# Attention: scores two units at a time, transposes one unit behind, context products between them

## The chip, the cores and the metric

The kernel runs on one core of a Trainium2 chip. The metric is the device time of one execution in microseconds (us), lower is better. Engines: PE is TensorE (matrix), with PEld for its weight loads; DVE is VectorE; ACT is ScalarE; POOL is GpSimd; SP issues the DMAs.

## The reference, cut to what matters

Four graph layers run one after another on 8 batch elements of 1024 nodes with 256 features. The change lies in the last one, attention with 8 heads of 32 features, in which the adjacency matrix (added to itself) multiplies the scores before the softmax:

```
q, k, v = proj(Wq, bq), proj(Wk, bk), proj(Wv, bv)          # [b, 8, 1024, 32]
scores = einsum('bhqd,bhkd->bhqk', q, k) * 32 ** -0.5
scores = scores * (adj + adj)[:, None, :, :]
attn = softmax(scores, axis=-1)
ctx = einsum('bhqk,bhkd->bhqd', attn, v)
x = layernorm(x + ctx @ Wo.T + bo)
```

## The kernel before, in words

The program treats the 8 batch elements one after another; each passes through the four layers, all on one core. Every engine has its own instruction list, written out by hand, and runs it in that order; semaphores tie the lists together. So the order of PE's work is the order of the Python loop in `@block.tensor`, and nothing reorders it.

In attention a *unit* is one query tile (128 rows, 8 tiles) of one head (8 heads): 64 units for an element, unit u being tile u // 8 and head u % 8. A unit's way:

- `scores` (L724): two matmuls of 512 columns on PE into two score banks. There are two such pairs of banks, used in turn, so unit u waits for `masked` of unit u - 2.
- DVE, L1530: one custom instruction multiplies the 128 x 1024 scores by the adjacency rows, writes them to one of three slots `r`, and gives their row maximum. POOL negates the maximum (L498).
- ACT, L1177: exponential in place, with the row sum.
- `transpose_p` (L734): eight transposes of 128 x 128 on PE into two banks, one for the lower four key tiles and one for the upper four. Each waits until its bank's copy of the unit before is done (`p_dve`, `p_act`).
- DVE L1546 copies the lower bank to `pt_0`, ACT L931 the upper one to `pt_1` or `pt_2`.
- `context` (L752): for a group of four heads, 16 small products per part, 32 instruction records, with the values; part 0 takes the lower keys, part 1 the upper ones. Groups 2 qt and 2 qt + 1 belong to query tile qt and both write bank 6 (the last group another). Before part 0 of the first group of a tile overwrites this bank, it waits for `c_raw`: DVE's product `c_f` (L1562) of the tile before.

Once per query tile there are also: the reciprocals of the row sums (DVE L1557), their spread over the partitions (`spread_denominators`, PE L765) and ACT's copy of it; `c_f` = context x spread reciprocals (DVE L1562); its split into high and low parts (ACT, POOL); the output projection (`output`, PE L506 to L508, bank 7); the residual addition into `xr` (DVE L1577), which needs the projection and waits for its own end; the statistics for the layer norm (DVE L1289, L1294); the normalisation (POOL, ACT), and the store.

Every engine's loop counts a step s. In PE's loop before, step s issues the scores of unit s + 1, the transposes of unit s - 2, part 0 of a group when s - 7 is a multiple of 4, part 1 when s - 9 is, the spread at s = 12, 20, ..., and the output projection at s = 16, 24, .... In steps 1 to 3 the values of two node tiles each are projected as well, between scores and transposes. DVE's step s has the masking product of unit s, in steps 1 to 3 the copy of the projected values (L1504), the copy of unit s - 2 (`LAG` is 2), the reciprocal at s = 8, 16, ..., `c_f` at s = 14, 22, ..., the residual addition at s = 17, 25, ..., and the statistics at s = 18, 26, .... ACT's step has the copy of unit s - 2, then the exponential of unit s. After the loop's last units PE already transposes adjacency tiles of the next element (L595).

Of the kernel before, what the change touches and what calls it, by code (L numbers as in the profile page):

```python
# [22 lines left out]
def build_program(nc: bass.Bass, d: dict, out: bass.AP):  # L23
# [7 lines left out]
    G = P // HD  # L31
    UNITS = NT * H
    EPS_DEG, EPS_ROW, EPS_LN = 1e-6, 1e-12, 1e-5
    SLOPE = 0.2
    LAG = 2
# [53 lines left out]
    with ExitStack() as ctx:  # L89
# [194 lines left out]
        def nth(b, per, n):  # L284

            return b * per + n
# [216 lines left out]
        def _(pe):  # L503
# [83 lines left out]
            def transpose_adj(b, j, half):  # L587

                n = tp["adj", j, half]
                tp_wait(b, n)  # L590
                for t in range(TPH):
                    i = TPH * half + t
                    if j == 0:
                        pe.wait_ge(adj_in[i], nth(b, 16, 16))
                    last = pe.transpose(tp_bank(n)[:, t * P:(t + 1) * P], adjn[:, i, j * P:(j + 1) * P], ident)  # L595
                last.then_inc(tp_full, 1)
# [50 lines left out]
            def project_pairs(b, name, w, rows_ready, pairs=range(PAIRS)):  # L647

                for k in pairs:
                    pe.wait_ge(*rows_ready(k))  # L650
                    dst = pr_bank(b, pr[name, k])
                    for s in range(2):
                        last = project(dst[:, s * F:(s + 1) * F], w, 2 * k + s)
                    last.then_inc(pr_full, 1)
# [19 lines left out]
            def xt_wait(b, layer):  # L674
                return lambda k: (tp_free, nth(b, TP_UNITS, x_ready(layer, 2 * k + 1)))
# [15 lines left out]
            def copied(b, n):  # L691

                pe.wait_ge(copies_dve if n % 2 else copies_act, nth(b, 2 * G, n // 2 + 1))

            def stack_copies(b, n):

                h, m, half = COPIES[n]
                pe.wait_ge(pr_free, nth(b, PR_UNITS, pr["qk", (0, m, half)] + 1))
                if 4 <= n < 3 * G or n >= 3 * G + 2:
                    copied(b, n - (4 if n < 3 * G else 2))  # L700
                at = slice(half * 512, (half + 1) * 512)
                block = lambda k, count: placer[:, (4 * h + k) * HD:(4 * h + k + count) * HD]
                dst = copies_bank(n)
                if m == 0:
                    pe.matmul(dst, block(2, 3), qk0_hi[:, 0, at], start=True, stop=False)
                    last = pe.matmul(dst, block(0, 3), qk0_lo[:, 0, at], start=False, stop=True)
                else:
                    pe.matmul(dst, block(1, 3), qk0_hi[:, 1, at], start=True, stop=False)
                    last = pe.matmul(dst, block(3, 3), qk0_lo[:, 1, at], start=False, stop=True)
                last.then_inc(copies_full, 1)  # L710

            def scores(b, u):
                qt, h = divmod(u, H)
                if u == 0:
                    copied(b, 3 * G - 2)
                    copied(b, 3 * G - 1)
                if u < G:
                    copied(b, 3 * G + u)
                if G <= u < 2 * G:
                    pe.wait_ge(stacked[u - G], nth(b, 16 * 6, 16 * 6))  # L720
                if u >= 2:
                    pe.wait_ge(masked, nth(b, UNITS, u - 1))
                for half in range(HALVES):
                    last = pe.matmul(ps[:, 2 * (u % 2) + half, :], q_stack[0:STACK, h, qt * P:(qt + 1) * P],  # L724
                                     k_stack[0:STACK, h, half * 512:(half + 1) * 512], start=True, stop=True)
                last.then_inc(s_full, 1)

            def transpose_p(b, u):
                pe.wait_ge(exp_done, nth(b, UNITS, u + 1))
                for half in range(HALVES):  # L730
                    if u >= 1:
                        pe.wait_ge(p_dve if half == 0 else p_act, nth(b, UNITS, u))
                    for t in range(TPH):
                        last = pe.transpose(ps[:, TP + half, t * P:(t + 1) * P],  # L734
                                            r[:, u % RSLOTS, (TPH * half + t) * P:(TPH * half + t + 1) * P], ident)
                    last.then_inc(p_full, 1)

            def context(b, grp, part):

                qt, g = divmod(grp, 2)  # L740
                if part == 0:
                    pe.wait_ge(p_dve, nth(b, UNITS, G * grp + G))
                    if grp == 0:
                        pe.wait_ge(pr_free, nth(b, PR_UNITS, PR_UNITS))
                    elif g == 0:
                        pe.wait_ge(c_raw, nth(b, NT + 1, qt))
                else:
                    pe.wait_ge(p_act, nth(b, UNITS, G * grp + G))
                for kt in range(TPH * part, TPH * (part + 1)):
                    for hh in range(G):  # L750
                        h = g * G + hh
                        last = pe.matmul(ps[HD * hh:HD * (hh + 1), ctx_bank(grp), g * P:(g + 1) * P],  # L752
                                         xn[:, kt, h * HD:(h + 1) * HD], p_half(grp * G + hh, kt // TPH)[:, kt % TPH, :],
                                         start=(kt == 0), stop=(kt == NT - 1), tile_position=(0, HD * hh))
                last.then_inc(ctx_done if part else ctx_half, 1)

            def spread_denominators(b, qt):

                pe.wait_ge(rp_ready, nth(b, NT, qt + 1))
                if qt >= 1:  # L760
                    pe.wait_ge(h_sum, nth(b, NT, qt))
                for g in range(2):
                    for hh in range(G):
                        h = g * G + hh
                        last = pe.matmul(ps[HD * hh:HD * (hh + 1), 7, g * P:(g + 1) * P],  # L765
                                         rprow[:, qt % 2, h:h + 1].broadcast_to([P, HD]), ident[:, :],
                                         start=True, stop=True, tile_position=(0, HD * hh))
                last.then_inc(rbc_full, 1)

            def output(b, qt):  # L770
                for g in range(2):
                    pe.wait_ge(c_ready, nth(b, NT + 1, NT + g if qt == NT - 1 else qt + 1))
                    last = three(ps[:, 7, 0:F], c_hi[:, g, :], c_lo[:, g, :], w_hi[:, W_O, g, :], w_lo[:, W_O, g, :],
                                 g == 0, g == 1)
                last.then_inc(o_full, 1)
# [4 lines left out]
            for b in range(B):  # L780
# [121 lines left out]
                    stack_copies(b, n)  # L902
                scores(b, 0)
                for s in range(UNITS + 10):
                    if s + 1 < UNITS:
                        scores(b, s + 1)
                    if s == 0:
                        for n in range(3 * G + 2, 4 * G):
                            stack_copies(b, n)
                    if 1 <= s < PAIRS:  # L910
                        project_pairs(b, "values", W_V, xt_wait(b, 3), range(s, s + 1))
                    if LAG <= s < UNITS + LAG:
                        transpose_p(b, s - LAG)
                    for part in range(2):
                        grp, late = divmod(s - 7 - 2 * part, G)
                        if late == 0 and 0 <= grp < 2 * NT:
                            context(b, grp, part)
                    if s in (UNITS + 1, UNITS + 5) and b + 1 < B:
                        for j in ((0, 1) if s == UNITS + 1 else (2, 3)):
                            transpose_adj(b + 1, j, 0)  # L920
                    if s >= 12 and (s - 12) % H == 0 and (s - 12) // H < NT - 1:
                        spread_denominators(b, (s - 12) // H)
                    if s == UNITS + 2:
                        spread_denominators(b, NT - 1)
                    if s >= 16 and (s - 16) % H == 0 and (s - 16) // H < NT:
                        output(b, (s - 16) // H)
# [274 lines left out]
        def _(dve):  # L1201
# [41 lines left out]
            def x_late_transposed(b, layer, part):  # L1243
                for (n, lo, src), (_, hi, _) in zip(x_late(layer, part, xt_lo), x_late(layer, part, xt_hi)):
                    dve.wait_ge(tp_hi, nth(b, TP_UNITS, n + 1))
                    rest(lo, src, hi, tp_free)
# [359 lines left out]
```

## Time and profile before

| | us |
|---|---|
| median of 3 runs | 3124.4 (3123.82 to 3126.77) |
| profiled execution | 3123.78 |
| its span, first to last instruction | 3122.0 |
| PE busy | 3021.2 (97%) |
| DVE busy | 2089.0 (67%) |
| ACT busy | 1718.1 (55%) |
| mean granted TensorE clock | 0.996 of full speed |

The busy time of an engine is summed over its instructions; matmuls are pipelined, and their ends are modelled. The chain that ended last goes from the last instruction backwards, at each step to what released it; groups in it are counted from the end of the one before to their own end, and so leave no overlap. Durations in the order of time overlap, since a matmul's weight load and its start lie beside the one before.

### The profile page before, as it was taken

To read this page: it belongs to the slowest core of one execution; us is meant where nothing else is said; L and a number is where in the kernel's file an instruction comes from. 1 tells how busy PE (TensorE), PEld (TensorE's weight loads), DVE (VectorE), ACT (ScalarE), POOL (GpSimd) and SP (SyncE) were. 2 spreads that over 40 slices of the span, in tenths; PEclk is the share of its full clock that TensorE was granted. 3 is DMA by queue.
4 is the path that set the end of the run, shared out by engine and by line. 5 is a ranking of instruction groups with operands and counts; after the bars stand their busy time and mean duration, and the time that the engine had idled before them with its cause. 6 is when DMAs were issued, how large, how long until landed. Compare 5 with 4: busy or idle time off the path is not lost.

```text
span 3122.0 us, 71133 instructions
## 1 busy us (share of the span) xinstructions
PE 3021.2 (97%) x28188; PEld 2645.0 (85%) x28188; DVE 2089.0 (67%) x4060; ACT 1718.1 (55%) x3048; POOL 448.6 (14%) x1666
## 2 busy tenths in 40 slices
PE   6999999999999999999999999999999999999999
PEld 5988889887898788987889977898778987789877
DVE  4637976379762797627976389753887538874388
ACT  3525854258542684526854278533785337853377
POOL 0101211012110121101211112111121111211112
PEclk9999999999999999999999999999999999999999
DMA  6022131121321213302133021330213302133110
GB/s 219 30 80 65 49 146 51 60 70 44 144 78 37 67 52 136 103 15 67 49 136 109 13 70 44 134 109 14 69 53 125 109 17 70 49 126 109 27 40 19
DMA packets 145270, 234.50 MB, mean 75 GB/s; under 512 B 12839, under 2 KB 113964, under 8 KB 144940
## 3 DMA queue, kind: packets, MB, share of 16 engines
q1 hardware_dynamic: 144940, 229.96, 22.7%
q8 instruction: 225, 3.69, 0.5%
q14 instruction: 105, 0.86, 0.1%
HBM read 120.86 MB, written 83.89 MB: 66 GB/s over the span
## 4 chain that ended last, share of the span: by engine, by line
PE 87%; DVE 5%; ACT 3%; SPq 2%; issue 1%; POOL 1%; DMA 0%; DVEq 0%; POOLq 0%; ACTq 0%
PE ps L506 17%; PE ps L508 16%; PE ps L507 16%; PE ps L734 15%; PE ps L724 9%; PE ps L752 8%; DVE t_lo L1233 2%; SPq L409 1%; PE ps L605 1%; PE ps L765 1%; PE ps L564 1%; ACT t_hi L931 1%; PE ps L595 1%; DVE xt_lo L1240 0%; DVE stats L1289 0%
## 5 line engine op out<-in xcount | busy, mean ns | idle before, releaser
L1530 DVE CUSTOM_DVE_ANT_0 r<-ps,adjn 128x1024 f32<-128x1024 f32 x512 | 620.7, 1212 | 19.0 <-DVE xr L1577 10.3
L1177 ACT ACTIVATE r<-r,nmax 128x1024 f32<-128x1024 f32 x512 | 584.8, 1142 | 23.0 <-POOL nmax L498 22.8
L506 PE MATMUL ps<-u_hi,t_hi 128*128 128x256 f32 x2048 | 588.6, 287 | 2.4 <-DVE t_lo L1233 1.8
L508 PE MATMUL ps<-u_hi,t_lo 128*128 128x256 f32 x2048 | 579.4, 283 | 0.0
L507 PE MATMUL ps<-u_lo,t_hi 128*128 128x256 f32 x2048 | 578.9, 283 | 0.0
L734 PEld LDWEIGHTS ps<-ident,r 128*128 128x128 f32 x4096 | 462.5, 141 | 116.0 <-issue 78.1
L734 PE MATMUL ps<-ident,r 128*128 128x128 f32 x4096 | 536.7, 274 | 7.9 <-DVE pt L1546 7.5
L1546 DVE COPY pt<-ps 128x512 f32<-128x512 f32 x512 | 352.9, 689 | 93.6 <-PE ps L734 74.2
L931 ACT ACTIVATE pt<-ps 128x512 f32<-128x512 f32 x512 | 304.0, 594 | 176.6 <-PE ps L734 160.4
L506 PEld LDWEIGHTS ps<-u_hi,t_hi 128*128 128x128 f32 x2048 | 391.4, 191 | 6.2 <-DVE t_lo L1233 6.2
L507 PEld LDWEIGHTS ps<-u_lo,t_hi 128*128 128x128 f32 x2048 | 391.4, 191 | 0.0
L508 PEld LDWEIGHTS ps<-u_hi,t_lo 128*128 128x128 f32 x2048 | 391.2, 191 | 0.0
L724 PE MATMUL ps<-k_stack,q_stack 96*128 96x512 f32 x1024 | 363.3, 437 | 6.1 <-ACT k_stack L931 4.3
L1006 ACT ACTIVATE xn<-y,shift,rstd 128x256 f32<-128x256 f32 x192 | 115.6, 602 | 456.8 <-POOL shift L474 456.0
L506 PE MATMUL ps<-w_hi,xt_hi 128*128 128x256 f32 x1152 | 334.4, 290 | 18.5 <-DVE xt_lo L1240 8.7
L507 PE MATMUL ps<-w_lo,xt_hi 128*128 128x256 f32 x1152 | 323.1, 280 | 0.0
L508 PE MATMUL ps<-w_hi,xt_lo 128*128 128x256 f32 x1152 | 322.7, 280 | 0.0
L467 POOL TENSOR_TENSOR vare<-mv,eps_ln 128x1 f32<-128x1 f32 x256 | 53.5, 209 | 1589.9 <-DVE mv L1294 1589.9
L752 PE MATMUL ps<-pt,xn 128*32 128x128 f32 x8192 | 274.9, 275 | 0.0
L1233 DVE TENSOR_TENSOR xt_lo<-ev,xt_hi 128x512 fp32r<-128x512 f32 x64 | 44.3, 693 | 316.4 <-ACT xt_hi L931 316.4
L506 PEld LDWEIGHTS ps<-w_hi,xt_hi 128*128 128x128 f32 x1152 | 218.5, 190 | 36.5 <-issue 13.4
L498 POOL TENSOR_TENSOR nmax<-zero,mmax 128x1 f32<-128x1 f32 x512 | 97.1, 190 | 1036.7 <-DVE mmax L1530 991.2
(164 smaller groups left out, 5235.8 us busy)
## 6 DMA issues: line engine op xcount, KB each, us to landing
adjn<-in_adj SPq DMA_DIRECT2D x64, 512.0 KB, 3.5
t_spill<-t_hi SPq DMA_DIRECT2D x64, 512.0 KB, 5.8
t_spill<-t_lo SPq DMA_DIRECT2D x64, 512.0 KB, 5.9
t_hi<-t_spill SPq DMA_DIRECT2D x32, 1024.0 KB, 5.3
t_lo<-t_spill SPq DMA_DIRECT2D x32, 1024.0 KB, 8.3
xn<-in_x SPq DMA_DIRECT2D x16, 512.0 KB, 4.5
x_spill<-xn SPq DMA_DIRECT2D x64, 128.0 KB, 1.7
q_stack<-u_hi SPq DMA_DIRECT2D x64, 128.0 KB, 2.5
```

Source lines behind the costliest of these rows:

```text
L506: pe.matmul(dst, a_hi, b_hi, start=first, stop=False, skip_group_check=check)
L507: pe.matmul(dst, a_hi, b_lo, start=False, stop=False, skip_group_check=check)
L508: return pe.matmul(dst, a_lo, b_hi, start=False, stop=last, skip_group_check=check)
L724: last = pe.matmul(ps[:, 2 * (u % 2) + half, :], q_stack[0:STACK, h, qt * P:(qt + 1) * P], k_stack[0:STACK, h, half * 512:(half + 1) * 512 ...
L734: last = pe.transpose(ps[:, TP + half, t * P:(t + 1) * P], r[:, u % RSLOTS, (TPH * half + t) * P:(TPH * half + t + 1) * P], ident)
L752: last = pe.matmul(ps[HD * hh:HD * (hh + 1), ctx_bank(grp), g * P:(g + 1) * P], xn[:, kt, h * HD:(h + 1) * HD], p_half(grp * G + hh, kt // ...
L931: copy = lambda dst, src, scale=1.0: nc.scalar.activation(dst, src, ACT.Copy, scale=scale)
L1006: act.activation(dst, src, ACT.Identity, bias=shift[:, t % 4:t % 4 + 1], scale=rstd[:, t % 4:t % 4 + 1]).then_inc(ln_done, 1)
L1177: act.activation(r[:, s % RSLOTS, :], r[:, s % RSLOTS, :], ACT.Exp, bias=nmax[:, s % 4:s % 4 + 1], accum_out=prow[:, qt % 2, h:h + 1]).the ...
L1233: dve.tensor_tensor(dst, value, f32(hi), ALU.subtract).then_inc(done, 1)
L1530: dve.tensor_tensor_reduce(out=r[:, s % RSLOTS, :], in0=ps[:, 2 * (s % 2):2 * (s % 2) + 2, :].rearrange("p a c -> p (a c)"), in1=adjn[:, q ...
L1546: dve.tensor_copy(p_half(u, 0).rearrange("p t q -> p (t q)"), ps[:, TP, :]).then_inc(p_dve, 1)
```

## The change

Only PE's instruction order in the attention loop is different. Scores are issued for two units in each odd step (s + 1 and s + 2; in step 0 for unit 1), the transposes are those of unit s - 1 instead of s - 2, and the context parts stand two steps earlier (s - 5 and s - 7 multiples of 4). A pair of steps before was: scores, transposes, scores, transposes, context. After, it is: scores, scores, transposes, context; transposes. The spread and the output projection keep their step numbers, and so do all lists of the other engines.

```diff
                 scores(b, 0)
                 for s in range(UNITS + 10):
-                    if s + 1 < UNITS:
-                        scores(b, s + 1)
+                    for u in (1,) if s == 0 else (s + 1, s + 2) if s % 2 else ():
+                        if u < UNITS:
+                            scores(b, u)
                     if s == 0:
                         for n in range(3 * G + 2, 4 * G):
                             stack_copies(b, n)
                     if 1 <= s < PAIRS:
                         project_pairs(b, "values", W_V, xt_wait(b, 3), range(s, s + 1))
-                    if LAG <= s < UNITS + LAG:
-                        transpose_p(b, s - LAG)
+                    if 1 <= s <= UNITS:
+                        transpose_p(b, s - 1)
                     for part in range(2):
-                        grp, late = divmod(s - 7 - 2 * part, G)
+                        grp, late = divmod(s - 5 - 2 * part, G)
                         if late == 0 and 0 <= grp < 2 * NT:
                             context(b, grp, part)
```

## Rows read from the trace of the kernel before

**Rows 1.** The page: busy time of the engines; shares of the chain by engine.

```profile
PE 3021.2 (97%) x28188; PEld 2645.0 (85%) x28188; DVE 2089.0 (67%) x4060; ACT 1718.1 (55%) x3048; POOL 448.6 (14%) x1666
PE 87%; DVE 5%; ACT 3%; SPq 2%; issue 1%; POOL 1%; DMA 0%; DVEq 0%; POOLq 0%; ACTq 0%
```

**Rows 2.** Busy time in one stretch: PE, PEld, DVE, ACT, POOL, granted clock, DMA.

```profile
350.00:400.00 50.00, 50.00 (x675) 39.64 (x674) 45.40 (x84) 42.14 (x79) 11.34 (x41) 1.00 0.12 39
```

**Rows 3.** Chain of waits, one block of 8 units: start us, us, what.

```profile
305.61 0.57 PE ps L765 x16
306.18 0.66 PE ps L724 x2
306.84 0.87 PE ps L734 x8
307.71 1.01 PE ps L752 x32
...
310.26 0.47 PE ps L724 x2
310.73 1.04 PE ps L734 x8
...
314.32 0.12 PE ps L506
...
315.03 0.47 PE ps L724 x2
...
316.38 1.01 PE ps L752 x32
...
323.02 0.57 PE ps L765 x16
```

**Rows 4.** Order of time, a later block: start us, us, engine, line, what, idle before.

```profile
344.68 0.69 DVE L1546 COPY pt<-ps 128x512 f32<-128x512 f32 x1 [0.72 <-PE ps L734]
...
345.29 0.41 DVE L1562 TENSOR_TENSOR c_f<-ps,rbc 128x256 f32<-128x256 f32 x1
345.49 0.86 PEld L734 LDWEIGHTS ps<-ident,r 128*128 128x128 f32 x8 [0.38 <-issue]
...
345.62 1.22 DVE L1530 CUSTOM_DVE_ANT_0 r<-ps,adjn 128x1024 f32<-128x1024 f32 x1
...
346.52 1.08 PE L752 MATMUL ps<-pt,xn 128*32 128x128 f32 x32
...
346.76 0.69 DVE L1546 COPY pt<-ps 128x512 f32<-128x512 f32 x1
...
347.37 1.22 DVE L1530 CUSTOM_DVE_ANT_0 r<-ps,adjn 128x1024 f32<-128x1024 f32 x1
...
351.39 0.42 DVE L1577 TENSOR_TENSOR xr<-ps,xr 128x256 f32<-128x256 f32 x1
...
352.02 1.22 DVE L1530 CUSTOM_DVE_ANT_0 r<-ps,adjn 128x1024 f32<-128x1024 f32 x1 [0.21 <-DVE xr L1577]
...
353.94 0.42 DVE L1289 BATCH_NORM_STATS2 stats<-xr 128x6 f32<-128x256 f32 x1
...
354.78 1.23 DVE L1530 CUSTOM_DVE_ANT_0 r<-ps,adjn 128x1024 f32<-128x1024 f32 x1
```

**Rows 5.** Element 1, first units and last: order of time, then chain.

```profile
664.91 1.21 DVE L1530 CUSTOM_DVE_ANT_0 r<-ps,adjn 128x1024 f32<-128x1024 f32 x1
...
664.48 0.73 PE ps L724 x2
...
666.57 0.47 PE ps L724 x2
...
787.48 1.01 PE ps L752 x32
...
803.07 0.87 PE ps L734 x8
...
804.95 0.60 PE ps L595 x4
```

## The prediction

> **What bounds the kernel now.** I read four views. First the engine shares of the page and the chain that ended last: the matrix engine (PE) is busy for 97% of the span and carries 87% of the chain [rows 1]. The reader should see from this only that PE decides on average. Second, one 50 us stretch inside the attention loop: PE is busy for all of it, but the vector engine (DVE) for 45.40 of 50 us [rows 2]. DVE is nearly full, so a faster PE soon meets it. Third, the chain of waits over one block of 8 units (one query tile) [rows 3]. Only PE groups stand in it, and one block takes 323.02 - 305.61 = 17.41 us. Fourth, the order of time on DVE, where the waits of the new order must be looked for [rows 4].
>
> I write S for the scores of a unit, T for its eight transposes, C for a context visit (x32), M for DVE's masking product and D for DVE's copy of the lower half of the transposed unit. From end to end, as the chain counts, S costs 0.47 after T and 0.66 after the spread (0.66 after C too), T costs 0.87 after S, C 1.01, the spread 0.57, and the output projection 6 x 0.12 = 0.72 [rows 3]. In the old order a pair is S T S T C, and the second T takes 1.04 instead of 0.87 [rows 3]: its weight load stands idle for 0.38 us until the copy D of the unit before is through, since D starts at 344.68, ends at 345.37, and T's loads begin at 345.49 [rows 4]. From D's end to T's end I count 1.21 (0.15 to the first matmul, 1.06 for it). A D can start 0.40 before T's end, when the first four transposes are out.
>
> DVE's pace: after M starts, D can start 1.14 later (345.62, 346.76), and the next M 0.61 after that (347.37). A unit needs 1.75. Per block come 0.33 for the context's scaling c_f (345.29 to 345.62), 0.63 for the residual add xr, which waits for its own end (351.39 to 352.02), 0.84 for the statistics (353.94 to 354.78) [rows 4], and about 0.11 for the reciprocal: 14.0 + 1.9 = 15.9 of 17.41 us. M's result is readable 1.21 after its start, by its duration.
>
> **The change part by part.** Nothing is removed or added; PE's instructions are reordered, and the other engines keep their order. A pair becomes S S T C T. No DMA is moved.
>
> *The order itself.* An S directly behind an S: 0.46, two of the 512-column matmuls, by half the S group of 0.47 [rows 3]; ends 0.40 and 0.50. T behind C is not in the loop of before; after C, the first four transposes of the next adjacency tile take 0.60 [rows 5], against 0.43 for half of T, so T would cost 0.87 + 0.17 = 1.04. Its ends are 0.87 (no switch cost) and 1.06 (the one T behind C at the element's end, which also had a copy to wait for, and so is an upper end). An undisturbed pair is then 0.47 + 0.46 + 0.87 + 1.01 + 1.04 = 3.85 us; a block of four is 15.40, plus 0.57 + 0.19 for the spread and the slower S behind it, plus 0.72 output: 16.88, a gain of 0.53 on 17.41. It comes from D hiding behind C, and not from fewer visits: the drop in C-to-S cost comes back in C-to-T.
> The Trainium skill (TensorEngine Tiling (Array Packing), Tiling Modes, Key Properties) says that changing the tiling mode drains the engine. The 0.17 above agrees. Entering and leaving C happens once per pair in both orders, so by that rule there is no switch saved, and the sum stays; without it the block would be 4 x 0.17 = 0.68 shorter.
>
> *The wait that appears at C.* The first context visit of a query tile (units 13, 21, ... of PE's loop) writes the bank that DVE must have scaled for the tile before (c_raw). DVE does that in its own step 14, 22, ..., behind D of unit 12, 20. In the old order C came two transposes later and c_f had ended 0.8 us before it (345.70 against C at 346.52 [rows 4]). In the new order C stands directly behind T(12), the very transposes that D(12) copies. So C waits for M(14), D(12), c_f. Everything behind it on PE waits too, T(13) first.
>
> *The wait that appears at T.* The output projection now comes after T(15), not T(14). DVE's residual add waits for it, and until it is done M(18) cannot start. Statistics follow one step later, so DVE's extras fall together while PE has run ahead: T(18) must wait for D(17).
>
> Laid out by hand for one block, zero at the end of T(15), all prices from [rows 3, 4]. PE: output 0.72, S18 1.19, S19 1.65, T16 2.52, C 3.53, T17 4.57, S20 5.04. DVE: D15 at -0.33; xr waits for the output, 0.76 to 1.39; M18 1.39; D16 2.53; statistics 3.14; M19 3.98; D17 5.12 to 5.81. So T18 ends at 5.81 + 1.21 = 7.02 where 5.04 + 0.46 + 0.87 = 6.37 was possible: **+0.65**. Queued behind it on PE are C, T19 and the spread. C 8.03, T19 9.07, spread 9.64, S22 10.30, S23 10.76, T20 11.63. DVE: M22 10.34, D20 11.48, c_f 12.09 to 12.50. C starts 0.12 later and takes 1.08: 13.70 against 12.64: **+1.06**. Then T21 14.74, S24 and S25 15.67, T22 16.54, C 17.55, T23 18.59. A block is 18.59 us, **1.18 longer** (16.88 + 0.65 + 1.06). ScalarE keeps up: it is busy for 42.14 of 50 us at 2.18 us a unit [rows 2], so it needs some 1.8 us of a unit that will take 2.3.
>
> *The start of the stage.* Element 1: S(2) ends at 665.21, M(1) began at 664.91 [rows 5], so S(3), now in the same visit, waits for 666.12 and ends near 666.97. The value projections of 1.4 us each were between S and T; now T(1) comes before the third. But DVE's order asks for values(2) before D(0) and values(3) before D(1). So: values(1) 668.33, T0 669.20, values(2) 670.62, D0 671.27 to 671.96, T1 673.17; S4, S5, values(3) 675.52, DVE's value copy, D1 676.17, T2 678.07, T3 679.82. Four pairs later T11 ends at 695.22. In the kernel before it ended at 787.48 (end of T55 [rows 5]) less 5 x 17.41 less 8.67 (T11 to T15, 307.71 to 316.38 [rows 3]) = 691.76: **+3.46** for each element. In elements 0 and 3, where a DMA holds the first copies, this costs the same, since the value projection is as late as the DMA.
>
> *From T11 to T15:* 9.55 against 8.67 (with the wait at C, no extras yet): +0.88. *T15 to T55:* 5 x 1.18 = 5.90. *T55 to T63:* by the same layout 18.29 (T62 waits for D61, which C's wait made late) against 803.94 - 787.48 = 16.46 [rows 5]: +1.83. *Tail:* behind T63 now come the output (0.72) and C before the next element's adjacency transposes, where C alone stood: +0.72.
>
> Sum: 3.46 + 0.88 + 5.90 + 1.83 + 0.72 = 12.8 us for an element, 8 elements: **+102 us**. The profiled execution took 3123.78 us (span 3122.0), the median is 3124.4, within 0.02%; forecast 3226 us, +3.3%.
>
> **The rivals.** *A, PE's gain stands.* One mechanism: the wait of the second T on the single transpose bank goes, and PE's own work sets the pace. That holds if c_f is ready within 0.2 us of T20's end and D17 within its slack. Then a block is 16.88 and the start costs nothing: 8 x 0.53 = 4.2 us for an element, 3090 us. For it: PE is 97% busy and in the chain almost alone. Against: D(20) can start at the earliest when T(20) is half out, so c_f cannot end before 11.23 + 0.61 + 0.41 = 12.25, 0.6 behind T20 even with an idle DVE. Chance 0.07.
> *B, only the wait at C costs.* DVE has more slack than I count, and the start is hidden by the DMA or given back: 7 x 1.06 - 4.2 = +3.2 for an element, 3150 us. For it: DVE's 15.9 us fit into 18. Against: each extra sits at a fixed place in its order, and the start's waits follow from program order. Chance 0.12.
> *C, the two score banks filled together cost more.* M of the first unit cannot start before S behind T of the pair before, so DVE loses about 0.3 us in each pair and can't catch up after c_f; if that happens in each of the four pairs, a block is near 19.4 and the whole 3275 us. Against: DVE's needs per undisturbed pair are 3.50 of 3.85. Chance 0.07.
> *D, the reorder does nothing*: the second T's wait was all there was and is replaced by an equal one: 3124 us. Chance 0.03.
>
> **How the numbers follow.** Forecast 0.71. Its own bounds: T behind C at 0.87 takes some 28 x 0.17 x 8 = 38 us off, S behind S gives -15 to +10 us, the start halved -14. Downward these reach 3165, toward B; upward 3245, toward C. About 0.2 is left out. What a measurement of this kernel tells from no change is about 0.2%, 6 us. Faster: A 0.07 and a little of the rest, 0.08; within: 0.04; slower: 0.88.
>
> **What would show it.** In the profile after: PE's busy time drops within the loop; DVE's c_f becomes the releaser of C seven times an element, with about 1.1 us; D(17) before T(18) in five or six blocks, about 0.65; T behind D is otherwise without a wait; the period is 18.6; T behind C at 1.04; the first copy D(1) near 14 us behind S(0) instead of 9.7; DVE's residual add waits for the output projection. A period below 17.4, or C behind c_f with no wait, would prove me wrong.

## The result, and the profile after

| | before | after |
|---|---|---|
| median | 3124.1 us (4 runs, 3123.72 to 3126.77) | 3237.65 us (4 runs, 3232.26 to 3240.71) |
| ratio after / before | | 1.036, 95% interval 1.0347 to 1.0372 |
| profiled execution; span | 3123.78; 3122.0 | 3232.26; 3230.4 |

The changed kernel is 3.6% slower. Forecast were 3226 us (+102 us) in a range of 3165 to 3245; measured are +113.5 us by the medians, +108.4 by the spans.

The page of the changed kernel, busy times, to be set beside [rows 1]: PE works 5 us less, its weight loads 15 us more, ScalarE 14 and DVE 2 us more, and the instruction counts are the same. None of these comes near the 108 us by which the span is longer.

```profile
PE 3016.3 (93%) x28188; PEld 2659.9 (82%) x28188; DVE 2091.3 (65%) x4060; ACT 1732.0 (54%) x3048; POOL 445.9 (14%) x1666
```

The same stretch as in [rows 2] (busy us of PE, PEld, DVE, ACT, POOL; clock): PE, busy for all 50 us before, is now busy for 45.92. The clock is the same 1.00.

```profile
350.00:400.00 50.00, 45.92 (x617) 37.38 (x615) 42.23 (x79) 38.95 (x72) 9.34 (x34) 1.00 0.14 46
```

The chain of waits over one block of the changed kernel (start us, us, what), against [rows 3]. It runs from the output projection of one tile to that of the next:

```profile
357.64 0.12 PE ps L506
...
358.35 0.93 PE ps L724 x4
359.28 0.88 PE ps L734 x8
360.15 1.01 PE ps L752 x32
361.17 1.02 PE ps L734 x8
362.19 0.48 PE ps L724 x2
362.67 0.03 issue
...
362.77 0.10 DVE mmax L1531
...
362.91 0.74 PE ps L724 x2
363.65 1.02 PE ps L734 x8
364.67 1.01 PE ps L752 x32
365.68 1.02 PE ps L734 x8
366.70 0.57 PE ps L765 x16
367.28 1.13 PE ps L724 x4
368.41 0.89 PE ps L734 x8
...
369.39 0.18 DVE pt L1547
...
369.91 0.42 DVE c_f L1563
...
370.47 1.08 PE ps L752 x32
371.55 1.02 PE ps L734 x8
...
376.41 0.12 PE ps L506
```

A block is 376.41 - 357.64 = 18.77 us instead of 17.41. It holds both waits. At 362.67 PE has issued the first scores of a visit and waits for the masked unit 19, behind the statistics; the transposes of unit 18 then take 1.02, since they wait for a copy too. From 369.30 on it waits for DVE's copy and c_f before the context visit can start at 370.47, 1.17 us behind the transposes. The pair behind it, 371.55 onwards, has no such wait. DVE in the order of time around that second wait, against the rows of c_f in [rows 4]:

```profile
368.16 1.22 DVE L1531 CUSTOM_DVE_ANT_0 r<-ps,adjn 128x1024 f32<-128x1024 f32 x1 [1.16 <-PE ps L724]
369.31 0.69 DVE L1547 COPY pt<-ps 128x512 f32<-128x512 f32 x1
369.91 0.41 DVE L1563 TENSOR_TENSOR c_f<-ps,rbc 128x256 f32<-128x256 f32 x1
```

DVE itself stood idle for 1.16 us just before the product of unit 22, waiting for scores, and then had product, copy and c_f in a row ahead of PE. Idle time on one side and a queue on the other within 2 us: I read that as an order that doesn't fit, and not as an engine without room; e1 and e6 test it. Over the whole span the waits are (engine, line, for whom: us in total, times, longest):

```profile
PEld ps L752 <- DVE pt L1547: 78.3, 56, 1.4
PE ps L752 <- DVE c_f L1563: 66.6, 56, 1.2
PEld ps L724 <- DVE mmax L1531: 33.6, 48, 1.0
PE ps L734 <- DVE pt L1547: 33.1, 32, 1.5
```

56 is 7 tiles in 8 elements, 48 is 6 in 8. The first two rows are one wait, seen by the weight loads and by the matmuls.

### The profile page after: what moved, and what is told of

Same layout as the page of the kernel before. It is cut to its first block, busy times and chain, and to the rows that moved or that the text cites. A ratio compares the mean times of both kernels' runs of the same rounds, so it can differ in the third digit from the quotient of the medians.

```text
span 3230.4 us, 71133 instructions
## 1 busy us (share of the span) xinstructions
PE 3016.3 (93%) x28188; PEld 2659.9 (82%) x28188; DVE 2091.3 (65%) x4060; ACT 1732.0 (54%) x3048; POOL 445.9 (14%) x1666
## 4 chain that ended last, share of the span: by engine, by line
PE 86%; DVE 7%; issue 3%; ACT 3%; POOL 1%; SPq 0%; DVEq 0%; DMA 0%; POOLq 0%; ACTq 0%
PE ps L506 17%; PE ps L508 16%; PE ps L507 16%; PE ps L734 15%; PE ps L724 8%; PE ps L752 8%; PE ps L605 1%; DVE t_lo L1234 1%; PE ps L564 1%; PE ps L765 1%; PE ps L595 1%; DVE pt L1547 1%; ACT t_hi L932 1%; DVE c_f L1563 1%; PE ps L705 1%
## 5 line engine op out<-in xcount | busy, mean ns | idle before, releaser
L734 PE MATMUL ps<-ident,r 128*128 128x128 f32 x4096 | 547.3, 276 | 33.1 <-DVE pt L1547 33.1
L734 PEld LDWEIGHTS ps<-ident,r 128*128 128x128 f32 x4096 | 454.3, 141 | 129.9 <-issue 98.6
L506 PE MATMUL ps<-w_hi,xt_hi 128*128 128x256 f32 x1152 | 334.7, 291 | 17.8 <-DVE xt_lo L1241 7.7
L752 PE MATMUL ps<-pt,xn 128*32 128x128 f32 x8192 | 276.5, 275 | 66.6 <-DVE c_f L1563 66.6
L724 PE MATMUL ps<-k_stack,q_stack 96*128 96x512 f32 x1024 | 314.5, 420 | 25.5 <-DVE mmax L1531 21.2
L752 PEld LDWEIGHTS ps<-pt,xn 128*32 128x32 f32 x8192 | 210.3, 109 | 110.0 <-DVE pt L1547 78.3
```

Source lines behind the costliest of these rows:

```text
L506: pe.matmul(dst, a_hi, b_hi, start=first, stop=False, skip_group_check=check)
L734: last = pe.transpose(ps[:, TP + half, t * P:(t + 1) * P], r[:, u % RSLOTS, (TPH * half + t) * P:(TPH * half + t + 1) * P], ident)
```

## The experiments

The theory W of the expectations is that of the prediction: the time goes into waits that the order makes. The rivals are that DVE is too full to follow, or that PE's new order is slower in itself. Each ratio is to the kernel before, run beside it on the same chip (3123.7 us beside e1 to e4, 3123.8 us beside e5 to e7, on another chip). The changed kernel wasn't run again there: differences to it are to the 3237.65 us above, whose runs spread over 8.5 us. Where a difference of the profiled executions' spans is given, it is to its 3230.4 us.

**e1_cf_early.** On DVE and ScalarE:

```diff
+ DVE, start of step s:  if s in (14, 22, ...): wait rbc_ready, ctx_done; c_f = ps * rbc
  DVE: masking product of unit s; copy of unit s - 2
- DVE, behind them:      if s in (14, 22, ...): wait rbc_ready, ctx_done; c_f = ps * rbc
+ ACT, step 13, 21, ...: copy of rbc ahead of the exponential
- ACT, step 13, 21, ...: copy of rbc behind the exponential
```

> DVE scales the context (c_f) at the start of its step 14, 22, ..., ahead of the masking product instead of behind that step's copy, and ScalarE copies the spread reciprocals ahead of that step's exponential. PE's order is that of the changed kernel. Theory W (the time is lost in waits that the order itself makes: one at C behind c_f, one at T(18), one at the start): C's wait goes, 56 times some 1.2 us, the block falls from 18.77 to about 17.5 us, the time to 3165 us (3155 to 3180), still above the kernel before. Rival R (DVE is simply too full, and C is only where this shows): the wait comes back at the transposes behind C, at least half of it stays, 3200 us or more. Rival S (PE's new order is slower in itself, waits are a symptom): no clear change, 3230 us.

Measured: 3167.69 us (ratio to before 1.0141, interval 1.0126 to 1.0156), 70.0 us less than the changed kernel (64.9 by the spans). The chain shows the block from 353.88 to 371.42, 17.54 us; the context visit follows its transposes without a wait:

```profile
353.88 0.12 PE ps L506
...
364.66 0.88 PE ps L734 x8
365.53 1.01 PE ps L752 x32
...
371.42 0.12 PE ps L506
```

In the waits of this kernel the rows of L752 for the copy and for c_f are gone, and the 33.6 us in 48 times for the masked unit stand unchanged. So the wait didn't move on. DVE now waits for ScalarE's copy of the reciprocals (41.8 us in 56 times), and PE doesn't feel it. R and S fall.

**e5_stats_later.** The statistics of the first six tiles two steps later:

```diff
- DVE s in (18, 26, ...): tile_stats;  POOL u in (20, ...): norm_tile;  ACT s in (21, ...): normalise
+ DVE s in (20, 28, ...): tile_stats;  POOL u in (21, ...): norm_tile;  ACT s in (22, ...): normalise
```

> The changed kernel with the layer norm's statistics of a query tile on DVE two steps later (step 20, 28, ... instead of 18, 26, ...), POOL's and ScalarE's parts of it one step later, for the first six tiles; nothing else moved. Theory W: the statistics no longer stand between the copy of unit 16 and the product of unit 19, so the second scores and the transposes of unit 18 are ready in time; the wait of some 0.65 us (with the slower score visit 0.7) goes, 6 times in each of 8 elements: 31 to 34 us off 3237, 3205 us (3195 to 3215). The wait at C for c_f stays as it is. Rival (DVE is full: 0.84 us of work only moves its lateness two steps on, and the wait comes back at unit 20): 3230 to 3237 us.

Measured: 3202.77 us (1.0252, 1.0238 to 1.0266): 34.9 us less than the changed kernel (31.4 by the spans), for 31 to 34 expected. The 48 waits of the score loads for the masked unit are gone, those of the score matmuls are 8 instead of 56, and the wait at the context is as it was:

```profile
PE ps L754 <- DVE c_f L1567: 66.3, 56, 1.2
...
PE ps L726 <- DVE mmax L1535: 8.5, 8, 1.1
```

DVE's work is the same. What counted was where the 0.84 us stood.

**e6_two_waits.** Both edits.

> Both edits: c_f and the spread reciprocals early (as in e1_cf_early) and the statistics two steps later (as in e5_stats_later). Theory W: the two waits are independent, so the savings add; a block is PE's own 16.9 us (0.57 + 0.72 + 0.19 + 4 x 3.85), shorter than the 17.41 of the kernel before, and what is left above it is the start, T(62) and the tail: 3167.7 less 6 x 8 x 0.63 = 3137 us (3128 to 3147). Rival (DVE at 15.9 of 16.9 us cannot keep up once PE is free): block 17.3 or more, 3155 us.

Measured: 3134.36 us (1.0033, 1.002 to 1.0046); 3237.65 - 70.0 - 34.9 = 3132.8 would be the plain sum. So the two waits are independent. The loop's pair then runs at PE's own pace:

```profile
353.22 0.93 PE ps L726 x4
...
357.06 0.94 PE ps L726 x4
```

A pair is 357.06 - 353.22 = 3.84 us for 3.85 laid out. Still the kernel is slower than before by 0.3%: what remains is the start and the tail (in the table behind e7, 29 and 4 us above the kernel before, against 22 us that the rest gives back).

**e2_values.** In DVE's steps 2 and 3 the order of two copies, on top of the changed kernel:

```diff
-                    if 1 <= s < PAIRS:
+                    if s == 1:
                         values(s)
                     (copy of unit s - 2)
+                    if 2 <= s < PAIRS:
+                        values(s)
```

> In DVE's steps 2 and 3 the copy of the transposed unit stands ahead of the copy of the projected values; all else is the changed kernel. Theory W: T(1) no longer waits for the second value projection nor T(2) for the third; by laying out the first four units, T(3) ends 1.8 us earlier in an element whose first copies are not held by a DMA and about 1.2 us earlier where they are: 10 to 15 us in all, 3225 us. Rival (the start is absorbed later, since DVE and PE wait for each other anyway): under 3 us, 3235 us.

Measured: 3222.54 us (1.0315, 1.03 to 1.0331), 15.1 us less than the changed kernel by the medians, the upper end of what was expected. The traces give less: the spans differ by 10.1 us, and the eight starts (first scores to the end of T(11)) add up to 256.1 us instead of 266.4, with the rest unchanged. The other 5 us are not shown to come from the swap; the granted clock was 0.994 to 0.995 in these four runs and 0.989 to 0.993 in those of the changed kernel. In the changed kernel, element 1, the order of time is this (start us, us, engine, line, what, idle before):

```profile
684.13 0.68 DVE L1547 COPY pt<-ps 128x512 f32<-128x512 f32 x1
...
684.96 1.07 PE L734 MATMUL ps<-ident,r 128*128 128x128 f32 x8 [1.55 <-DVE pt L1547]
...
689.01 0.68 DVE L1547 COPY pt<-ps 128x512 f32<-128x512 f32 x1
689.84 1.06 PE L734 MATMUL ps<-ident,r 128*128 128x128 f32 x8 [1.47 <-DVE pt L1547]
```

The second copy starts 4.9 us behind the first, though its transposes ended at 686.02, because the value copy stands ahead of it and waits for a projection that PE does after them. With the two copies swapped the transposes of unit 3 end 16.5 us after the first scores of the element instead of 17.8, 1.3 us earlier where 1.8 was expected.

**e3_pairs_only.** One part of the change alone.

```diff
-                    if 1 <= s <= UNITS:
-                        transpose_p(b, s - 1)
+                    if LAG <= s < UNITS + LAG:
+                        transpose_p(b, s - LAG)
-                        grp, late = divmod(s - 5 - 2 * part, G)
+                        grp, late = divmod(s - 7 - 2 * part, G)
```

> One part of the change alone: scores of two units in one visit; transposes stay two units behind and the context where it was. Theory W: with three slots, the masking product of the second unit must wait for the transposes of the step before, and the second scores wait for that product: by hand a pair takes 0.47, then to 2.15, then 0.87 + 1.01 + 1.04 = 5.07 us against 4.35 in the kernel before (17.41 / 4); 256 pairs give +184 us: 3310 us (3270 to 3340). No wait at C for c_f. Rival (two scores in one visit save a switch, and the rest of the change spoils it): 3085 us.

Measured: 3477.62 us (1.1143, 1.1118 to 1.1168). The direction and the mechanism are W's, the size is 354 us instead of 184, outside the range I gave. The chain of one pair:

```profile
361.84 0.73 PE ps L724 x2
362.56 0.88 PE ps L734 x8
363.44 1.01 PE ps L752 x32
364.45 0.60 PE ps L734 x4
...
366.01 1.22 DVE r L1531
...
367.29 0.73 PE ps L724 x2
...
380.51 1.86 PE ps L752 x32
```

A pair is 5.45 us here; others are longer, and the mean block (T(15) to T(55), by five, all elements) is 23.4 us. I let the product start when the transposes end; but DVE's list has their copy (0.61) ahead of it, and once DVE is on the path in each pair, its extras (c_f here between 365.68 and 366.01) are no longer beside PE's work, but all added: 354 / 64 = 5.5 us a block, against 4 x 0.72 = 2.9 expected. The last row shows a second cause, which wasn't expected: the same context visit takes 1.86 us instead of 1.01, at half the granted clock, behind waits in which PE was busy for 2.05 of 4 us:

```profile
376.00:380.00 4.00, 2.05 (x12) 1.26 (x10) 2.60 (x7) 1.72 (x3) 1.16 (x5) 1.00 0.00 0
381.00:383.00 2.00, 2.00 (x31) 1.55 (x24) 0.94 (x2) 1.27 (x3) 0.19 (x1) 0.50 0.00 0
```

The columns are those of [rows 2]. The mean clock of this run was 0.976, against 0.996 in the profile of the kernel before. By these means 83 and 12 us of full-clock time were not granted, so by my estimate at most some 70 of the 354 us are the clock's. PE's waits carry the rest, and they come before the clock falls: the score matmuls alone wait for DVE 248 times, 242.7 us in all. As expected, no context visit waits for c_f here.

**e4_lag_only.** The other part alone.

```diff
-                    for u in (1,) if s == 0 else (s + 1, s + 2) if s % 2 else ():
-                        if u < UNITS:
-                            scores(b, u)
+                    if s + 1 < UNITS:
+                        scores(b, s + 1)
```

> The other part alone: transposes one unit behind and the context two steps earlier, scores one unit at a time (PE also waits for the last two stack copies before the first transposes, which changes nothing in time). Theory W: T of a unit waits for D of the unit before, and D comes behind M of the unit after, which needs the scores just issued: 3.25 us from those scores' end to T's end, but PE needs only 2.21 where no context lies between: about 1 us in each pair, and the wait at C for c_f stays (7 x 1.2 an element). A pair near 4.9 us: 3350 us (3280 to 3420). Rival (a shorter lag alone costs only at C): 3124 + 70 = 3195 us.

Measured: 3387.66 us (1.0842, 1.0826 to 1.0858), in the range of W. A block is 355.09 - 333.86 = 21.23 us (the spreads of two tiles in the chain). The waits of PE:

```profile
PE ps L737 <- DVE pt L1549: 146.8, 160, 1.9
...
PE ps L755 <- DVE c_f L1565: 77.1, 56, 1.4
```

The transposes wait for the single bank's copy 160 times, and the wait for c_f is there 56 times without paired scores. So it belongs to the shorter lag and not to the pairing, which alone (e3) doesn't have it. Each part alone costs more (264 and 354 us) than both together (114). As I read it, pairs of scores give the short lag something to run beside, and the short lag frees the slots that pairs need.

**e7_all.** e6 with e2's swap, and on PE:

```diff
+ steps 1 and 3: scores(s + 1), values(s), scores(s + 2) instead of both scores first
+ step UNITS + 1: the next element's adjacency transposes ahead of the context visit
```

> As e6_two_waits, and three more: DVE's value copies behind the transposed unit's (as in e2_values); in PE's steps 1 and 3 the value projection between the two scores, so that it does not stand behind the second scores' wait for a masked unit; and the next element's first adjacency transposes ahead of the context visit at the loop's end. Theory W: the start gives back 15 us (measured in e2_values) and another 0.9 us an element at S(3), the tail up to 1 us an element: 3137 - 15 - 7 - 6 = 3109 us (3098 to 3122), faster than the kernel before by 0.5%. Rival (start and tail are bound by DVE and DMA chains, the order on PE does not matter there): 3130 us, no faster than before.

Measured: 3106.05 us (5 runs, 3101.54 to 3110.27), ratio to before **0.9943**, interval 0.9931 to 0.9956. It is faster than both kernels, by 0.6% and 4.1%. One block in its chain is 348.34 - 331.49 = 16.85 us:

```profile
331.49 0.12 PE ps L508
...
348.34 0.12 PE ps L508
```

16.88 was laid out for PE alone.

The traces separate the start from the tail. From the order of time on PE, summed over the eight elements, in us of the profiled executions:

| | before | after | e2 | e6 | e7 |
|---|---|---|---|---|---|
| first scores to the end of T(11) | 242.0 | 266.4 | 256.1 | 271.2 | 246.4 |
| T(11) to T(15) | 69.2 | 77.7 | 77.6 | 67.9 | 67.9 |
| T(15) to T(55), five blocks | 696.7 | 751.0 | 751.0 | 674.2 | 674.3 |
| T(55) to T(63) | 132.1 | 148.1 | 148.0 | 133.8 | 133.8 |
| T(63) to the next element's first scores, or to the end | 1704.8 | 1709.8 | 1710.4 | 1709.1 | 1701.6 |

From e6 to e7 the start gives 24.8 us and the tail, which lies in the last row with the other three layers, 7.5 (the medians differ by 28.3 us, the spans by 33.7).

## Why the prediction was right

*What bounds.* PE on average, DVE close behind: confirmed by e6 and e7, where a block reaches PE's own 16.9 us with DVE's work unchanged. In the block DVE was not the bound; its order was.

*T behind C.* Taken at 1.04 from the adjacency transposes, measured 1.02. *Two scores in one visit* 0.93 together, for 0.47 + 0.46. The gain of 0.53 a block was real: 17.41 - 16.85 = 0.56, and it came, as the prediction said, from the copy that hides behind the context visit: in the undisturbed pair that follows 371.55 the copy runs from 374.41 to 375.10, beside the visit that ends at 375.38.

*The wait at C.* Predicted +1.06 a block, 56 times, of which 0.99 is PE's wait and 0.07 the slower visit behind it. The rows have 1.17 for the wait and 1.08 instead of 1.01 for the visit, together 1.24; e1 gives 1.25 by the medians (70.0 / 56) and 1.16 by the spans (64.9 / 56). The excess of 0.18 has a place: the product started 368.16, where 357.64 + 10.34 = 367.98 was laid out. DVE starts 0.21 us behind the end of a score group that the chain shows (after 358.35 + 0.47 the next product starts at 359.03), and I had counted 0.04, as for transposes. The Trainium skill (Perfetto Trace Analysis, Optimizing Tensor Performance, Matmuls) asks that independent groups rotate through PSUM banks, so that the emptying of one lies beside the next; all context groups but an element's last share one bank here, and the trace shows the wait that the rule warns of, 1.2 us each time. That a second bank would end it was not tried, since all eight are in use; e1 gets the same by emptying it sooner.

*The wait at T(18).* Laid out to end at 7.02, measured 364.67 - 357.64 = 7.03. Its share by e5 is 34.9 us by the medians and 31.4 by the spans, for 6 x 8 x 0.65 = 31. The prediction named the copy D(17) as the last cause; it does set the end of T(18) (362.77 + 0.69 + 1.21 = 364.67), but in the chain the first thing to be late is the second scores of the visit, which wait for the product of unit 19. Both are set by the same place, the statistics ahead of that product.

*The start.* Forecast +3.46 us for an element. In element 1 T(11) ends at 708.01 - 674.87 = 33.14 us behind the first scores, against 691.76 - 662.16 = 29.60: +3.54. *T11 to T15:* 9.72 us for 9.55. *Blocks:* 18.77 for 18.59. *T55 to T63:* 830.06 - 811.58 = 18.48 for 18.29. *Tail:* 832.38 - 830.06 = 2.32 against 1.61 [rows 5]: +0.71 for +0.72. The chain rows for the last three:

```profile
811.58 0.12 PE ps L506
...
830.06 0.12 PE ps L506
...
832.38 0.02 issue
```

Sum for element 1: 3.54 + 1.05 + 5 x 1.36 + 2.02 + 0.71 = 14.1 us, for 12.8 predicted. Eight times that would be 113 us, and that this is also the difference of the medians is chance: the trace it comes from is 108.4 us longer and not 113, and element 1 loses more at its start (3.54 us) than the elements do on average (3.05). Over all eight, by the table, the start cost 24.4 us where 27.7 were forecast, and everything from T(11) to T(63) cost 78.8 where 68.9 were. So two terms were mis-sized, in opposite directions. The block (and the stretches before and behind it) was 0.18 us too short 56 times, by the start of the product behind the scores. The start was too dear: the prediction let elements 0 and 3, where a DMA holds the first copies, lose as much as element 1, but they lose 2.5 and 2.3 us, and element 6 only 2.0; why that one does is open. By the spans the forecast is 6 us off, by the medians 11; that it isn't 10 by the spans owes to the two errors cancelling in part, which is luck.

*The rivals.* A (PE's gain stands) needed c_f within 0.2 us; it is 1.2 late. B had only the wait at C; e5 and e2 show 31 and 10 us elsewhere, by the spans. C wanted a late product in each of four pairs and no catching up; two pairs in a block are disturbed, each behind an extra of DVE, and in e6, with the same paired scores, the block is 16.85 us. A late product in each pair does happen in e3, where the slots tie product and transposes. D falls with the interval.

## What to carry to other kernels

When one engine's list is reordered, lay out one period of *all* lists with durations from the trace: each wait that was covered by the old distance shows up there with its place, and the sum came within 11 us of 113 by the medians, 6 of 108 by the spans, with two errors that partly cancelled. A busy share of 90% doesn't say that an engine cannot follow; look whether it idles just before it is late (1.16 us here), since then moving one instruction in its list (and here the copy that feeds it) gets the time back. Two edits that each look like part of an improvement can each be much worse alone, so test the parts only to find causes and not to judge them.

## What the runs showed of the hardware that was not expected

A wait of PE can cost more than its own length here, since the granted clock fell from full to half in short stretches; in the changed kernel most lie between the elements' attention loops, but one behind the waits of the new order. The profile lists busy us of PE, PEld, DVE, ACT and POOL, then the clock. This is the start of element 7 of the changed kernel, where PE waited for the copies of the transposed units:

```profile
3076.00:3080.00 4.00, 1.85 (x16) 1.47 (x15) 3.27 (x6) 0.90 (x4) 0.19 (x1) 1.00 0.00 0
3081.00:3083.00 2.00, 2.00 (x7) 1.56 (x6) 0.89 (x2) 1.42 (x2) 0.17 (x1) 0.50 0.00 0
```

PE was busy for 1.85 of 4 us, and the clock fell when the work was back; the four score matmuls at 3081.20 took 2.06 us, those at 3074.16 1.17. That start took 34.7 us, those of the other seven elements 33.1 to 33.2. Three starts of e6 are longer too (34.6 to 36.3 us), each with such a fall; no start of e2 or e7 has one.

Over the span the mean clock was 0.993 in the profiled execution (3232.26 us) and 0.989 in the slowest of the four (3240.71 us), 0.996 in the profile of the kernel before. The changed kernel's executions spread over 8.5 us, e2's over 0.9 us. The profiled execution is the fastest of the four, and that goes with the difference between 108.4 us by the spans and 113.5 us by the medians; that the clock causes it was not tested, since only one execution has a trace. In the kernel before clock and time hardly go together: its runs at 0.992 have spans of 3120.4 to 3124.4 us, those at 0.995 of 3119.6 to 3121.9.
